# Turning half of the attention probabilities on VectorE and by DMA in the second cross attention of a Perceiver block

## The chip, the cores and the metric

The kernel is one program on one core of a Trainium2 chip. The metric is device time in microseconds (us) of one execution. It is written in float32 and computes six layers one behind another; the change is in the fourth.

## The reference

The input is `x`, 128 batches of 32 tokens with 128 features, and a context of 128 batches of 257 rows. Six layers add to `x`; the one that is changed is the second cross attention. Layer normalisation of `x` gives the queries, keys and values come from the raw context, there are 16 heads of 8 features.

```python
Q = _split_heads(x_q @ W_q.T + b_q)          # x_q = layernorm(x): 128 x 32 x 128
K = _split_heads(x_k @ W_k.T + b_k)          # x_k = x_v = ctx_1024: 128 x 257 x 128
V = _split_heads(x_v @ W_v.T + b_v)
scores = jnp.einsum('bhqd,bhkd->bhqk', Q, K) / jnp.sqrt(jnp.float32(D_K))
scores = jnp.where(mask == 0, jnp.float32(-1000000000.0), scores)
attn = jax.nn.softmax(scores, axis=-1)
out = jnp.einsum('bhqk,bhkd->bhqd', attn, V)
...
return out @ W_o.T + b_o
```

## The kernel before

`xattn1` (from L1424) is the stage. After a short part that makes all queries, a pipeline runs over the 128 batches, one batch to a step. `run_steps` unrolls the first and last steps and loops over the rest, eight steps to a turn of the loop. Each engine has its own `step(g, j)`, with s = 8g + j the step's number; four steps are a tile of 128 tokens and b = j % 4 is the step's place in its tile. The order on an engine is the order in which `step` is written; engines wait for each other by counting semaphores.

One batch has 32 queries and 16 heads, that is 512 rows of scores. They lie as four groups of 128 partitions (4 heads by 32 queries), so the probabilities `prob` of a batch are 128 partitions by 4 groups by 257 keys. To multiply them by the values, the keys have to be on the partitions: the probabilities are turned. The work on batch n is spread over several steps, so in step s:

- TensorE (PE): `turn` (L1732) transposes the probabilities of batch s against the identity into PSUM, four groups for keys 0 to 127 into `turn_ps[0]` and four for keys 128 to 255 into `turn_ps[1]`; then the transposes of `weight` and of the raw context of batch s+4 into `in_ps`; `score` (L1721) for batch s+2; the keys (L1777) of batch s+3 into `turn_ps[0]` and its values (L1782) into `turn_ps[1]`; once a tile the output projection (L1789); last `values` (L1738) for batch s, four matmuls for each half of the keys, accumulated in `out_ps` on top of `last_part`, the share of key 256.
- VectorE (DVE): copies `turn_ps[0]` to `probT[:, 0]` (L1641); the reciprocals `rinv` of batch s+1 (L1646), for which it waits until all four exponentials of batch s+1 are done; if b is 0 the sum over heads `oT_sum` (L1650), if b is 2 the addition to `x` (L1655) and its statistics (L70); then `mask` (L1627) for groups 0 and 1 of batch s+2, which adds the mask to the scores and takes the minimum; `kT` (L1665) of batch s+3; `mask` for groups 2 and 3; and `own` (L1675), which picks each head's part of the output.
- ScalarE (ACT): copies `turn_ps[1]` to `probT[:, 1]` (L1693) and `in_ps` to `turned_in` (L1698); the exponentials of groups 0 and 1 of batch s+2 (L1686); the copy of the values `v` (L1707); the exponentials of groups 2 and 3. An exponential is two instructions, the second reads the row sum.
- GpSimd (POOL): the share of the last key (L1607) and `weight` (L1611) of batch s+1, and once a tile the queries spread over heads (L1594) and the mask as numbers (L1621).
- SyncE (SP): the DMAs. One `b_raw` of 128 KB a step (L1557), `b_kept` (L1561) and `b_v_rows` (L1565) once a tile each.

`turn_ps[1]` is shared: `turn(g, j, 1)` has to wait until ScalarE has copied `v` of the step before out of it (`v_ready`). `turn_ps[0]` is shared in the same way with the keys (`k_ready`).

Of the kernel before, what the change touches and what calls it, by code (L numbers as in the profile page):

```python
# [21 lines left out]
ACT = mybir.ActivationFunctionType  # L22
# [3 lines left out]
P = 128  # L26
# [1397 lines left out]
def xattn1(k, io):  # L1424
# [8 lines left out]
    with ExitStack() as stack:  # L1433
# [87 lines left out]
        rsum, rinv = sb("b_rsum", [P, 4, GROUPS]), sb("b_rinv", [P, 4, GROUPS])  # L1521
        probT = sb("b_probT", [P, 2, CH])
        last_part = sb("b_last_part", [P, 2, D])
# [5 lines left out]

        turn_ps = [psum("b_turn0"), psum("b_turn1")]  # L1530
        out_ps, in_ps = psum("b_out"), psum("b_in")
# [5 lines left out]
        scored, masked, exped, rinv_ready = (sem(f"b_{n}") for n in ("scored", "masked", "exped", "rinv_ready"))  # L1537
        turned, probT_ready = [sem(f"b_turned{n}") for n in range(2)], [sem(f"b_probT_ready{n}") for n in range(2)]
        out_ready, weight_ready, last_ready, own_ready, sum_ready, oT_ready, proj_ready, x_added = (
# [12 lines left out]
        with nc.Block() as block:  # L1552

            @block.sync
            def _(sp):
                def load_raw(g, j):
                    sp.dma_start(raw[:, j % 8], io["ctx_1024"][ds(g * 8 + j, 1), 0:2 * P, :].rearrange(  # L1557
                        "b (t p) d -> p (b t) d", p=P)).then_inc(raw_loaded[j % 8], 16)

                def load_kept(t, u):  # L1560
                    sp.dma_start(kept[:, u], k.keep1[ds(t * BPT, BPT), :].unsqueeze(0).broadcast_to([P, BPT, N_CTX]))\  # L1561
                        .then_inc(kept_loaded[u], 16)

# [62 lines left out]
            def _(dve):  # L1626
                def mask(g, j, grp):  # L1627
                    s, n, par = g * 8 + j, (j + 2) % 8, j % 2
                    if grp == 0:
# [5 lines left out]
                        scalar=3.4e38, op0=ALU.add, op1=ALU.min, accum_out=nmax[:, par, grp:grp + 1]).then_inc(masked, 1)  # L1635

                def step(g, j):
                    s, t, u, b = g * 8 + j, tile_of(g, j), j // 4, j % 4
                    if live(g, j, 0):
                        dve.wait_ge(turned[0], s + 1)  # L1640
                        nc.vector.tensor_copy(probT[:, 0, :], turn_ps[0][:]).then_inc(probT_ready[0], 1)  # L1641
                    if live(g, j, 1):
# [18 lines left out]
                    if live(g, j, 3):  # L1661
                        n = (j + 3) % 4
                        dve.wait_ge(k_done, s + 4)
                        dve.wait_ge(kept_loaded[(j + 3) // 4 % 2], (g + (j + 3) // 8 + 1) * 16)
                        nc.vector.scalar_tensor_tensor(kT[:, n, :], turn_ps[0][:, 0:N_CTX], k.bk1, kept[:, (j + 3) // 4 % 2, n, :],  # L1665
                                                       ALU.add, ALU.mult).then_inc(k_ready, 1)
# [15 lines left out]
            def _(act):  # L1682
# [6 lines left out]
                def step(g, j):  # L1689
                    s, t, u, b = g * 8 + j, tile_of(g, j), j // 4, j % 4  # L1690
                    if live(g, j, 0):
                        act.wait_ge(turned[1], s + 1)
                        nc.scalar.activation(probT[:, 1, :], turn_ps[1][:], ACT.Copy).then_inc(probT_ready[1], 1)  # L1693
                    if live(g, j, 4) or live(g, j, 0):
# [10 lines left out]
                    if live(g, j, 3):  # L1705
                        act.wait_ge(v_done, s + 4)
                        nc.scalar.activation(v[:, (j + 3) % 8], turn_ps[1][:, 0:2 * P].rearrange("p (t d) -> p t d", d=D), ACT.Copy)\  # L1707
                            .then_inc(v_ready, 1)
# [11 lines left out]
            def _(pe):  # L1720
# [10 lines left out]

                def turn(g, j, kt):  # L1732
                    for grp in range(GROUPS):
                        last = nc.tensor.transpose(turn_ps[kt][:, grp * P:(grp + 1) * P],  # L1734
                                                   prob[:, j % 4, grp, kt * P:(kt + 1) * P], k.ident[:])
                    last.then_inc(turned[kt], 1)

                def values(g, j, kt):  # L1738
                    s = g * 8 + j
                    pe.wait_ge(probT_ready[kt], s + 1)  # L1740
                    for grp in range(GROUPS):
                        rows = slice(grp * 32, grp * 32 + 32)
                        last = nc.tensor.matmul(out_ps[rows, 0:P], v[:, j, kt, rows], probT[:, kt, grp * P:(grp + 1) * P],
                                                start=False, stop=(kt == 1), skip_group_check=True)
                    return last

                def step(g, j):
                    s, t, u, b = g * 8 + j, tile_of(g, j), j // 4, j % 4
                    here, ahead = live(g, j, 0), live(g, j, 4)
                    if here:  # L1750
                        pe.wait_ge(exped, s * 4 + 4)
                        pe.wait_ge(k_ready, upto(g, s, 3))
                        turn(g, j, 0)
                        pe.wait_ge(v_ready, upto(g, s, 3))
                        turn(g, j, 1)
                    if here or ahead:
# [12 lines left out]
                    if live(g, j, 3):  # L1769
                        n = (j + 3) % 8  # L1770
                        pe.wait_ge(in_copied, s + 4)
                        if n % 4 == 0:
                            pe.wait_ge(keys_ready, tile_of(g, j, 3) + 1)
                        if here:
                            pe.wait_ge(probT_ready[0], s + 1)
                        wait(pe, k_ready, s + 3)
                        nc.tensor.matmul(turn_ps[0][:, 0:N_CTX], k.wk1[:], turned_in[:, n, C0:C0 + N_CTX], start=True, stop=True).then_inc(k_done, 1)  # L1777
                        if here:
                            pe.wait_ge(probT_ready[1], s + 1)
                        wait(pe, v_ready, s + 3)  # L1780
                        for kt in range(2):
                            last = nc.tensor.matmul(turn_ps[1][:, kt * D:(kt + 1) * D], turned_in[:, n, C0 + kt * P:C0 + (kt + 1) * P], k.wv1[:],  # L1782
                                                    start=True, stop=True)
# [746 lines left out]
```

## Time and profile before

| what | us |
|---|---|
| median of three runs | 2270.99 |
| lowest and highest run | 2270.51, 2272.9 |
| span of the profiled execution | 2270.1 |
| PE, DVE, ACT, POOL busy over the span | 1957.3, 1626.0, 1640.6, 899.0 |
| pipeline of the stage: first to last `b_rinv` | 1336.5 to 1825.5 |

The span is that of one profiled execution; the runs are timed without the profiler. Rows of a timeline have the start, the duration, the engine, the line, the operation, output and inputs, a count, and in brackets the idle time before it and what ended it. Start times of neighbours on one engine tell more than durations, because instructions overlap a little.

### The profile page before, as it was taken

Reading aid. Unit: us, or ns where it says so; the run is one execution under the profiler, and the core shown is the slowest. Engines: PE = TensorE matmul, PEld = TensorE weight load, DVE = VectorE, ACT = ScalarE, POOL = GpSimd, SP = SyncE. Lnnn points to the kernel's source line nnn. Section 1 sums busy time; section 2 is a strip of 40 time slices with the busy share of each in tenths; the row PEclk is TensorE's granted clock in tenths of the full one; section 3 lists DMA queues with packets and bytes.
Section 4 is the critical chain, followed back from the end, with each engine's and each line's share of the span. In section 5 each row is a group of like instructions: output and inputs, shape, how many; then the busy total and the mean of one; then the engine's idle time right before and its main releaser. Section 6 shows DMA issues by size and latency. Waiting matters only on the chain. (4 is left out here: it accounts for less than half of the span.)

```text
span 2270.1 us, 55792 instructions
## 1 busy us (share of the span) xinstructions
PE 1957.3 (86%) x15563; PEld 1549.6 (68%) x15563; DVE 1626.0 (72%) x5153; ACT 1640.6 (72%) x4441; POOL 899.0 (40%) x1338
## 2 busy tenths in 40 slices
PE   3799999999999999995350579999999989858997
PEld 3688888888888888883240257777777756526775
DVE  5677777777777777764778758888888878854564
ACT  3588888888888888876486368888888878735553
POOL 1533443444433333422245123333333357533554
PEclk8699999999999999997585789999999999969999
DMA  4211111111110111100000022222222100013222
GB/s 134 73 34 34 33 33 33 33 33 33 29 28 27 30 33 33 33 4 1 0 0 0 0 73 66 74 65 65 74 65 65 52 2 0 1 28 84 89 83 84
DMA packets 124106, 93.89 MB, mean 41 GB/s; under 512 B 14417, under 2 KB 101937, under 8 KB 123905
## 3 DMA queue, kind: packets, MB, share of 16 engines
q1 hardware_dynamic: 122550, 90.88, 14.6%
q10 hardware_dynamic: 1194, 1.58, 0.2%
q8 instruction: 34, 0.56, 0.1%
q0 software_dynamic: 288, 0.56, 0.1%
q14 instruction: 40, 0.32, 0.0%
HBM read 88.26 MB, written 4.72 MB: 41 GB/s over the span
## 5 line engine op out<-in xcount | busy, mean ns | idle before, releaser
L750 ACT ACTIVATE a_prob<-a_neg,a_nmax 128x289 f32<-128x289 f32 x512 | 270.5, 530 | 79.0 <-DVE a_nmax L679 72.9
L1686 ACT ACTIVATE b_prob<-b_neg,b_nmax 128x257 f32<-128x257 f32 x512 | 255.2, 500 | 71.2 <-DVE b_nmax L1633 71.1
L645 POOL TENSOR_TENSOR a_xn<-a_z,g 128x256 f32<-128x256 f32 x128 | 93.3, 729 | 526.3 <-DVE a_z L705 526.3
L807 PE MATMUL a_score<-a_xnT,a_qT 128*128 128x290 f32 x1536 | 274.8, 315 | 1.1 <-DVE a_qT L726 1.1
L835 PE MATMUL a_out<-a_probT,a_xn 128*128 128x256 f32 x1024 | 263.6, 380 | 0.3 <-DVE a_probT L690 0.3
L679 DVE CUSTOM_DVE_ANT_0 a_neg<-a_score,a_bias 128x289 f32<-128x289 f32 x512 | 222.0, 459 | 46.4 <-PE a_score L807 40.0
L807 PEld LDWEIGHTS a_score<-a_xnT,a_qT 128*128 128x128 f32 x1536 | 216.5, 191 | 43.8 <-issue 43.2
L1633 DVE CUSTOM_DVE_ANT_0 b_neg<-b_score,b_bias 128x257 f32<-128x257 f32 x512 | 195.9, 421 | 50.8 <-PE b_score L1729 48.6
L755 ACT ACTIVATE a_prob<-a_prob,a_rinv 128x256 f32<-128x256 f32 x512 | 230.4, 499 | 1.1 <-DVE a_rinv L717 1.0
L835 PEld LDWEIGHTS a_out<-a_probT,a_xn 128*128 128x128 f32 x1024 | 175.0, 191 | 13.6 <-DVE a_probT L690 0.6
L1607 POOL TENSOR_TENSOR b_last_part<-b_v_rows,b_prob 128x128 f32<-128x128 f32 x128 | 52.0, 406 | 318.2 <-ACT b_prob L1686 318.2
L735 DVE TENSOR_TENSOR a_xnT<-a_ctx,a_xnT 128x256 fp32r<-128x256 f32 x128 | 54.4, 425 | 159.7 <-ACT a_xnT L786 159.7
L2396 POOL TENSOR_TENSOR m_hidden<-m_full,m_hidden 128x512 fp32r<-128x512 f32 (+1 forms) x88 | 114.2, 1298 | 107.2 <-ACT m_hidden L2377 107.2
L1734 PE MATMUL b_turn<-ident,b_prob 128*128 128x128 f32 x1024 | 144.5, 281 | 1.4 <-DVE b_kT L1665 0.7
L854 PE MATMUL a_q<-latT,A 128*128 (+1 forms) x1024 | 139.8, 281 | 6.4 <-DVE a_qT L726 4.1
L854 PEld LDWEIGHTS a_q<-latT,A 128*128 128x128 f32 x1024 | 131.2, 197 | 7.8 <-DVE a_qT L726 5.1
L817 PE MATMUL a_turn<-ident,a_prob 128*128 128x128 f32 x1024 | 132.7, 273 | 0.8 <-ACT a_prob L755 0.7
L1734 PEld LDWEIGHTS b_turn<-ident,b_prob 128*128 128x128 f32 x1024 | 108.9, 141 | 33.5 <-ACT b_prob L1686 14.4
L876 PE MATMUL a_ctx<-U,a_oT 128*128 128x128 f32 x1024 | 119.7, 275 | 0.7 <-ACT a_oT L791 0.7
L817 PEld LDWEIGHTS a_turn<-ident,a_prob 128*128 128x128 f32 x1024 | 118.8, 141 | 1.4 <-ACT a_prob L755 1.4
L2372 ACT ACTIVATE m_silu<-m_g 128x512 f32<-128x512 f32 (+1 forms) x88 | 52.6, 598 | 90.2 <-PE m_g L2026 90.2
L876 PEld LDWEIGHTS a_ctx<-U,a_oT 128*128 128x128 f32 x1024 | 116.9, 192 | 1.1 <-ACT a_oT L791 1.1
(479 smaller groups left out, 5192.2 us busy)
## 6 DMA issues: line engine op xcount, KB each, us to landing
a_raw<-in_ctx SPq DMA_DIRECT2D x128, 128.0 KB, 3.4
b_raw<-in_ctx SPq DMA_DIRECT2D x128, 128.0 KB, 3.3
m_wide<-expert_weights SPq DMA_DIRECT2D x128, 128.0 KB, 2.9
a_kept<-keep SPq DMA_DIRECT2D x32, 257.0 KB, 3.9
b_kept<-keep SPq DMA_DIRECT2D x32, 257.0 KB, 3.5
b_v_rows<-ctx_tail_values SPq DMA_DIRECT2D x32, 256.0 KB, 3.6
a_tail<-latents_normalised SPq DMA_DIRECT2D x64, 64.0 KB
latents_normalised<-lat_affine SPq DMA_DIRECT2D x8, 256.0 KB, 2.3
```

What stands on the lines that cost most here:

```text
L679: nc.vector.tensor_tensor_reduce(out=neg[:, grp, :], in0=score_ps[grp % 2][:, 0:KEYS0], in1=bias[:, n, :], scale=-DH0 ** -0.5, scalar=3.4e ...
L750: nc.scalar.activation(prob[:, par, grp, :], neg[:, grp, :], ACT.Exp, bias=nmax[:, par, grp:grp + 1], scale=-1.0, accum_out=rsum[:, par, g ...
L755: return nc.scalar.activation(part, part, ACT.Copy, scale=rinv[:, (j + 1) % 2, grp:grp + 1])
L807: last = nc.tensor.matmul(score_ps[grp % 2][:, 0:even(KEYS0)], qT[:, a, un, bn, 4 * grp:4 * grp + 4, :], xnT[:, c, n, :], start=(p == 0), ...
L817: last = nc.tensor.transpose(turn_ps[kt][:, grp * P:(grp + 1) * P], prob[:, j % 2, grp, kt * P:(kt + 1) * P], k.ident[:])
L835: nc.tensor.matmul(out_ps[:, half, 0:2 * P], xn[:, j, kt, :], probT[:, kt, half * 2 * P:(half + 1) * 2 * P], start=(kt == 0), stop=False)
L854: last = nc.tensor.matmul(q_ps[:, h * P:(h + 1) * P], k.A[:, 4 * hg + h, :], k.latT[:, ds((t + ahead) * P, P)], start=True, stop=True)
L876: last = nc.tensor.matmul(proj_ps, oT[:, h, :], k.U[:, h, :], start=(h == 0), stop=(h == H - 1))
L1633: nc.vector.tensor_tensor_reduce(out=neg[:, par, grp, :], in0=score_ps[grp][:, 0:N_CTX], in1=bias[:, n, :], scale=-DH1 ** -0.5, scalar=3.4 ...
L1686: nc.scalar.activation(prob[:, n, grp, :], neg[:, par, grp, :], ACT.Exp, bias=nmax[:, par, grp:grp + 1], scale=-1.0, accum_out=rsum[:, n, ...
L1734: last = nc.tensor.transpose(turn_ps[kt][:, grp * P:(grp + 1) * P], prob[:, j % 4, grp, kt * P:(kt + 1) * P], k.ident[:])
L2396: nc.gpsimd.tensor_tensor(h[0:r1, LO, :], full[0:r1, 1 - u, :], h[0:r1, HI, :], ALU.subtract).then_inc(lo_ready, 1)
```

## The change

For keys 0 to 127 the four transposes on TensorE and VectorE's copy of them go. In their place VectorE transposes the 16 blocks of 32 by 32 of the probabilities in SBUF with one instruction (`turn_blocks`), and SyncE issues four DMAs of 64 KB that spread each head's 32 partitions over all 128 (`spread_prob`). The key with the number 4c + r goes through row c of block r, so VectorE reads `prob` with a distance of four elements (16 bytes) between neighbours, and writes runs of 32. This is done for batch s+1 in step s, ahead of the reciprocals. Keys 128 to 255 stay as they were. The keys' projection gets a PSUM bank of its own (`k_ps`), and TensorE's waits for VectorE's copy go.

```diff
-        probT = sb("b_probT", [P, 2, CH])
+        blocks, spreadT = sb("b_blocks", [P, 2, 4, GROUPS, L]), sb("b_spreadT", [P, 2, 4, GROUPS, L])
+        probT = sb("b_probT", [P, CH])
...
+                def spread_prob(g, j):
+                    s, n = g * 8 + j, (j + 1) % 2
+                    sp.wait_ge(blocks_ready, s + 2)
+                    wait(sp, out_ready, s)
+                    for i in range(4):
+                        sp.dma_start(spreadT[:, n, i].rearrange("p g l -> p (g l)"),
+                                     blocks[i * L:(i + 1) * L, n].rearrange("c r g l -> c r (g l)")).then_inc(spreadT_loaded[n], 16)
+
...
+                    if live(g, j, 1):
+                        spread_prob(g, j)
...
+                def turn_blocks(g, j):
...
+                    s, n = g * 8 + j, (j + 1) % 2
+                    dve.wait_ge(exped, s * 4 + 8)
+                    wait(dve, out_ready, s)
+                    nc.vector.transpose(blocks[:, n].rearrange("p r g l -> p g r l"),
+                                        prob[:, (j + 1) % 4, :, 0:P].rearrange("p g (c r) -> p g r c", r=4)).then_inc(blocks_ready, 1)
+
...
-                    if live(g, j, 0):
-                        dve.wait_ge(turned[0], s + 1)
-                        nc.vector.tensor_copy(probT[:, 0, :], turn_ps[0][:]).then_inc(probT_ready[0], 1)
+                    if live(g, j, 1):
+                        turn_blocks(g, j)
...
                 def values(g, j, kt):
-                    s = g * 8 + j
-                    pe.wait_ge(probT_ready[kt], s + 1)
+                    if kt == 0:
+                        pe.wait_ge(spreadT_loaded[j % 2], (g * 4 + (j // 2 + 1)) * 64)
+                    else:
+                        pe.wait_ge(probT_ready, g * 8 + j + 1)
...
                         pe.wait_ge(exped, s * 4 + 4)
-                        pe.wait_ge(k_ready, upto(g, s, 3))
-                        turn(g, j, 0)
                         pe.wait_ge(v_ready, upto(g, s, 3))
-                        turn(g, j, 1)
+                        turn(g, j)
```

VectorE, from the end of a step to the first mask of the next, a step with b = 2. The ISA rows on L1633 (L1645 after) are the mask and the read of its minimum. Before:

```order
L1675 TENSOR_TENSOR b_own<-b_out,b_turned_in 128x128
L1641 COPY b_probT<-b_turn 128x512
L1646 RECIPROCAL b_rinv<-b_rsum 128x4
L1655 TENSOR_TENSOR x<-b_out,x 128x128
L70 BN_STATS stats<-x 128x6
L1633 ISA b_neg,b_nmax<-b_score,b_bias 128x257
```

After:

```order
L1695 TENSOR_TENSOR b_own<-b_out,b_turned_in 128x128
L1655 STREAM_TRANSPOSE b_blocks<-b_prob 128x4x4x32
L1666 RECIPROCAL b_rinv<-b_rsum 128x4
L1675 TENSOR_TENSOR x<-b_out,x 128x128
L70 BN_STATS stats<-x 128x6
L1645 ISA b_neg,b_nmax<-b_score,b_bias 128x257
```

The block transpose stands where the copy stood; it reads `prob` of batch s+1, which ScalarE writes, and no longer a PSUM bank that TensorE writes.

TensorE, one step, before:

```order
L1734 MATMUL b_turn<-ident,b_prob 128x128 x8
L1760 MATMUL b_in<-ident,b_weight 128x128
L1765 MATMUL b_in<-ident,b_raw 128x128 x2
L1729 MATMUL b_score<-b_kT,b_qbd 128x257 x4
L1777 MATMUL b_turn<-b_turned_in,wk1T 128x257
L1782 MATMUL b_turn<-wv1T,b_turned_in 128x128 x2
L1795 MATMUL b_out<-ident,b_last_part 128x128
L1743 MATMUL b_out<-b_probT,b_v 32x128 x8
```

After:

```order
L1754 MATMUL b_turn<-ident,b_prob 128x128 x4
L1780 MATMUL b_in<-ident,b_weight 128x128
L1785 MATMUL b_in<-ident,b_raw 128x128 x2
L1749 MATMUL b_score<-b_kT,b_qbd 128x257 x4
L1795 MATMUL b_k<-b_turned_in,wk1T 128x257
L1800 MATMUL b_turn<-wv1T,b_turned_in 128x128 x2
L1813 MATMUL b_out<-ident,b_last_part 128x128
L1764 MATMUL b_out<-b_spreadT,b_v 32x128 x4
L1764 MATMUL b_out<-b_probT,b_v 32x128 x4
```

Four transposes are gone at the head of the step, and the first four of `values` take `spreadT`.

SyncE, a step with b = 1, before:

```order
L1557 DMA b_raw<-in_ctx 128x2x128
L413 ISA
L1561 ISA
L1561 DMA b_kept<-keep 128x1028
L413 REGISTER_ALU
```

After:

```order
L1559 DMA b_raw<-in_ctx 128x2x128
L1572 REGISTER_ALU
L1575 DMA b_spreadT<-b_blocks 128x1x128 x4
L413 ISA
L1563 ISA
L1563 DMA b_kept<-keep 128x1028
```

The four DMAs stand between a step's `b_raw` and the tile's loads.

## Rows read from the trace of the kernel before

**Rows 1.** Windows: busy us of each engine, granted PE clock, DMA share, GB/s.
```profile
1160.00:1170.00 10.00, 7.15 (x32) 5.60 (x30) 8.63 (x5) 7.14 (x13) 1.29 (x1) 1.00 0.00 0
1500.00:1800.00 300.00, 299.58 (x3310) 224.40 (x3303) 252.80 (x991) 256.96 (x875) 108.83 (x234) 1.00 0.26 67
1970.00:1980.00 10.00, 7.98 (x145) 4.79 (x143) 8.28 (x22) 6.09 (x15) 3.13 (x2) 1.00 0.01 2
1990.00:2000.00 10.00, 8.73 (x32) 5.72 (x32) 7.60 (x28) 4.18 (x8) 0.00 (x0) 0.50 0.00 0
```

**Rows 2.** Waits, 1360 to 1800 us: total us, times, longest.
```profile
ACT b_prob L1686 <- DVE b_nmax L1633: 63.2, 114, 0.8
DVE b_neg L1633 <- PE b_score L1729: 40.8, 58, 0.7
...
PEld b_turn L1734 <- ACT b_v L1707: 2.5, 15, 0.2
```

**Rows 3.** Timeline of ScalarE: the first exponential of five steps in a row.
```profile
1599.56 0.51 ACT L1686 ACTIVATE b_prob<-b_neg,b_nmax 128x257 f32<-128x257 f32 x1 [0.57 <-DVE b_nmax L1633]
...
1603.45 0.51 ACT L1686 ACTIVATE b_prob<-b_neg,b_nmax 128x257 f32<-128x257 f32 x1 [0.69 <-DVE b_nmax L1633]
...
1607.20 0.51 ACT L1686 ACTIVATE b_prob<-b_neg,b_nmax 128x257 f32<-128x257 f32 x1 [0.25 <-DVE b_nmax L1633]
...
1611.16 0.51 ACT L1686 ACTIVATE b_prob<-b_neg,b_nmax 128x257 f32<-128x257 f32 x1 [0.64 <-DVE b_nmax L1633]
...
1614.93 0.51 ACT L1686 ACTIVATE b_prob<-b_neg,b_nmax 128x257 f32<-128x257 f32 x1 [0.57 <-DVE b_nmax L1633]
```

**Rows 4.** Timeline: last row sum of a batch to the next mask, b = 0.
```profile
1601.72 0.19 ACT L1686 ACTIVATION_READ_ACCUMULATOR b_prob<-b_neg,b_nmax 128x1 f32 x1
...
1601.94 0.18 DVE L1646 RECIPROCAL b_rinv<-b_rsum 128x4 f32<-128x4 f32 x1
...
1602.04 1.04 DVE L1650 TENSOR_REDUCE b_oT_sum<-b_own 128x128 f32<-128x512 f32 x1
...
1603.00 0.42 DVE L1633 CUSTOM_DVE_ANT_0 b_neg<-b_score,b_bias 128x257 f32<-128x257 f32 x1
```

**Rows 5.** Timeline of VectorE: reciprocals and first mask, b = 2.
```profile
1609.71 0.17 DVE L1646 RECIPROCAL b_rinv<-b_rsum 128x4 f32<-128x4 f32 x1
...
1610.69 0.43 DVE L1633 CUSTOM_DVE_ANT_0 b_neg<-b_score,b_bias 128x257 f32<-128x257 f32 x1
```

**Rows 6.** Timeline: `v` copy, transposes and VectorE's copy at a step's head.
```profile
1612.16 0.36 ACT L1707 ACTIVATE b_v<-b_turn 128x256 f32<-128x256 f32 x1
1612.16 1.09 PE L1734 MATMUL b_turn<-ident,b_prob 128*128 128x128 f32 x8
...
1612.86 0.69 DVE L1641 COPY b_probT<-b_turn 128x512 f32<-128x512 f32 x1
...
1613.09 0.27 PE L1760 MATMUL b_in<-ident,b_weight 128*128 128x128 f32 x1
...
1613.54 0.18 DVE L1646 RECIPROCAL b_rinv<-b_rsum 128x4 f32<-128x4 f32 x1
```

**Rows 7.** Groups of VectorE over 512 elements: busy us, mean ns, idle.
```profile
L1650 DVE TENSOR_REDUCE b_oT_sum<-b_own 128x128 f32<-128x512 f32 x32 | 33.4, 1045 | 0.0
...
L1908 DVE TENSOR_REDUCE s_rsum<-s_expd 128x16 f32<-128x512 f32 x32 | 21.5, 671 | 0.2
```

**Rows 8.** The DMAs of L1557 and the one of 64 KB: duration, landing.
```profile
L1557 SPq DMA_DIRECT2D b_raw<-in_ctx x128: 372/373/470, 1324.1 to 1790.9; - x128
...
DMA to landing us min/median/max: 2.6/3.3/5.2
...
ctx_tail_values<-b_v_tail SPq DMA_DIRECT2D x1, 64.0 KB, 1.6
```

**Rows 9.** The last reciprocals and the last `values` of the pipeline.
```profile
1825.49 0.18 DVE L1646 RECIPROCAL b_rinv<-b_rsum 128x4 f32<-128x4 f32 x1 [0.39 <-ACT b_prob L1686]
...
1828.21 0.77 PE L1743 MATMUL b_out<-b_probT,b_v 128*32 128x128 f32 x16
```

More of the change, by code:

```diff
@@ L1528, in xattn1 @@
         score_ps = [psum(f"b_score{g}") for g in range(GROUPS)]
-        turn_ps = [psum("b_turn0"), psum("b_turn1")]
+        k_ps, turn_ps = psum("b_k"), psum("b_turn")
         out_ps, in_ps = psum("b_out"), psum("b_in")
@@ L1537, in xattn1 @@
         scored, masked, exped, rinv_ready = (sem(f"b_{n}") for n in ("scored", "masked", "exped", "rinv_ready"))
-        turned, probT_ready = [sem(f"b_turned{n}") for n in range(2)], [sem(f"b_probT_ready{n}") for n in range(2)]
+        turned, probT_ready = sem("b_turned"), sem("b_probT_ready")
+        blocks_ready, spreadT_loaded = sem("b_blocks_ready"), [sem(f"b_spreadT_loaded{u}") for u in range(2)]
         out_ready, weight_ready, last_ready, own_ready, sum_ready, oT_ready, proj_ready, x_added = (
@@ L1664, in step @@
                         dve.wait_ge(kept_loaded[(j + 3) // 4 % 2], (g + (j + 3) // 8 + 1) * 16)
-                        nc.vector.scalar_tensor_tensor(kT[:, n, :], turn_ps[0][:, 0:N_CTX], k.bk1, kept[:, (j + 3) // 4 % 2, n, :],
+                        nc.vector.scalar_tensor_tensor(kT[:, n, :], k_ps[:, 0:N_CTX], k.bk1, kept[:, (j + 3) // 4 % 2, n, :],
                                                        ALU.add, ALU.mult).then_inc(k_ready, 1)
@@ L1691, in step @@
                     if live(g, j, 0):
-                        act.wait_ge(turned[1], s + 1)
-                        nc.scalar.activation(probT[:, 1, :], turn_ps[1][:], ACT.Copy).then_inc(probT_ready[1], 1)
+                        act.wait_ge(turned, s + 1)
+                        nc.scalar.activation(probT[:], turn_ps[:], ACT.Copy).then_inc(probT_ready, 1)
                     if live(g, j, 4) or live(g, j, 0):
@@ L1706, in step @@
                         act.wait_ge(v_done, s + 4)
-                        nc.scalar.activation(v[:, (j + 3) % 8], turn_ps[1][:, 0:2 * P].rearrange("p (t d) -> p t d", d=D), ACT.Copy)\
+                        nc.scalar.activation(v[:, (j + 3) % 8], turn_ps[:, 0:2 * P].rearrange("p (t d) -> p t d", d=D), ACT.Copy)\
                             .then_inc(v_ready, 1)
@@ L1730, in score, with turn @@
                     last.then_inc(scored, 1)
-                def turn(g, j, kt):
+                def turn(g, j):
                     for grp in range(GROUPS):
-                        last = nc.tensor.transpose(turn_ps[kt][:, grp * P:(grp + 1) * P],
-                                                   prob[:, j % 4, grp, kt * P:(kt + 1) * P], k.ident[:])
-                    last.then_inc(turned[kt], 1)
+                        last = nc.tensor.transpose(turn_ps[:, grp * P:(grp + 1) * P], prob[:, j % 4, grp, P:2 * P], k.ident[:])
+                    last.then_inc(turned, 1)
                 def values(g, j, kt):
-                    s = g * 8 + j
-                    pe.wait_ge(probT_ready[kt], s + 1)
+                    if kt == 0:
+                        pe.wait_ge(spreadT_loaded[j % 2], (g * 4 + (j // 2 + 1)) * 64)
+                    else:
+                        pe.wait_ge(probT_ready, g * 8 + j + 1)
                     for grp in range(GROUPS):
                         rows = slice(grp * 32, grp * 32 + 32)
-                        last = nc.tensor.matmul(out_ps[rows, 0:P], v[:, j, kt, rows], probT[:, kt, grp * P:(grp + 1) * P],
+                        last = nc.tensor.matmul(out_ps[rows, 0:P], v[:, j, kt, rows],
+                                                spreadT[:, j % 2, :, grp, :] if kt == 0 else probT[:, grp * P:(grp + 1) * P],
                                                 start=False, stop=(kt == 1), skip_group_check=True)
@@ L1773, in step @@
                             pe.wait_ge(keys_ready, tile_of(g, j, 3) + 1)
+                        wait(pe, k_ready, s + 3)
+                        nc.tensor.matmul(k_ps[:, 0:N_CTX], k.wk1[:], turned_in[:, n, C0:C0 + N_CTX], start=True, stop=True).then_inc(k_done, 1)
                         if here:
[L1775 to L1779, printed above, removed]
+                            pe.wait_ge(probT_ready, s + 1)
                         wait(pe, v_ready, s + 3)
                         for kt in range(2):
-                            last = nc.tensor.matmul(turn_ps[1][:, kt * D:(kt + 1) * D], turned_in[:, n, C0 + kt * P:C0 + (kt + 1) * P], k.wv1[:],
+                            last = nc.tensor.matmul(turn_ps[:, kt * D:(kt + 1) * D], turned_in[:, n, C0 + kt * P:C0 + (kt + 1) * P], k.wv1[:],
                                                     start=True, stop=True)
```

## The prediction

> **What bounds the kernel now.** I read the windows first. In the pipeline of the stage TensorE looks full: 299.58 of 300 us busy at a granted clock of 1.00 [rows 1]. That alone would say that four transposes fewer a batch are pure gain. So I read the waits next [rows 2]: ScalarE waits in each step for VectorE's minimum (63.2 us in 114 steps), VectorE in half of the steps for TensorE's scores (40.8 us in 58), and TensorE at times for ScalarE's copy of `v` (2.5 us in 15). Each of the three waits for another, so the thing to look for is closed loops that pass through several engines. I measure a step from one first exponential to the next [rows 3]: 3.89 us into b = 0, 3.75 into b = 1, 3.96 into b = 2, 3.77 into b = 3; together 15.37, 3.84 a batch. Two loops matter.
>
> *Loop 1, ScalarE and VectorE.* From the first exponential (1599.56 [rows 3]) to the end of the last row sum of the batch is 2.35 us (1601.72 + 0.19 [rows 4]). 0.03 later come the reciprocals, 0.10 after their start the sum over heads, 0.96 after that the first mask (1603.00), and 0.45 later the first exponential of the next step. That is 3.89, exactly the step into b = 0: there VectorE is never idle, and this loop is the bound. Without the sum over heads the same loop is 2.35 + 0.03 + 0.10 + 0.47 = 2.95. With b = 2 the addition to `x` and its statistics stand between reciprocals and mask, 0.98 instead of 0.10 [rows 5], so it is 3.83.
>
> *Loop 2, through all three.* The `v` copy starts 1.00 us after the first exponential and ends at 1612.52; TensorE's eight transposes start at 1612.16 and the next transpose follows at 1613.09, that is 0.117 each [rows 6]. The fifth, the first that needs `v` to be out of its bank, is due at 1612.63, only 0.11 after the copy ends. TensorE's queue and this loop are thus almost equally long; the queue decides the steps into b = 1, 2 and 3 (3.96 is the one with the projection in it).
>
> **What the change takes away.** Four transposes are 4 x 0.117 = 0.47 us of TensorE's queue. But in loop 2 little of it comes back: the four that stay may start when the copy ends, 1612.52 + 0.03, they need 0.47, and the next transpose stands at 1613.02 instead of 1613.09. The loop is 3.77 - 0.07 = 3.70. So the gain is at most 0.07 in an ordinary step, and in the step into b = 2, where the projection no longer shows, 3.96 - 3.70 = 0.26. VectorE's copy goes too; it took 0.68 from start to start [rows 6], but it ran while VectorE was waiting for the last exponential anyhow (1612.86 to 1613.54, with the row sum done only shortly before).
>
> **What it adds on VectorE.** The block transpose of batch s+1 needs all four exponentials of that batch, as the reciprocals do, and stands ahead of them. It can't start before the last row sum, and behind it in VectorE's queue stand the reciprocals, the extra work and the first mask, for which ScalarE waits. So its whole time T goes into loop 1, in every step. This is the new wait: an operation that waited for a bank that was ready early is replaced by one that waits for the latest event of the step. The loops become 2.95 + T (b = 1 and 3), 3.89 + T (b = 0) and 3.83 + T (b = 2).
>
> How long is T? No block transpose is in the trace. The low bound is the copy of the same 512 elements, 0.68. The nearest row that reads SBUF at a distance is the sum over heads, also 512 elements, neighbours 32 elements apart: it takes 1045 ns against 671 for a sum over as many contiguous elements [rows 7], and 0.96 from start to start [rows 4]. The transpose reads four elements apart. I take 0.96, since that row shares the unusual thing, the distance, and keep 0.68 for the low end. The high end is half the copy's rate, 2 x 0.68 = 1.36, my estimate.
>
> The pages disagree here. The Trainium skill (SBUF — State Buffer, the note on cachelines) says that SBUF is read in lines of 16 bytes and that each access that goes on to a new line pays; reads 16 bytes apart do so each time, which would give the slow value and 2339 us; it also names four fp32 as how far one may stride for free, which is just this distance, so it can be read either way. The Trainium skill (Vector Engine (DVE) Microarchitecture Reference, on `transpose_mode`) says that the 32x32 transpose sustains one element per cycle per lane, which would give the fast value and 2308 us. Rows 7 fit the first for a sum and show nothing of a transpose.
>
> **What it adds as DMA.** Four issues a batch on SyncE; an issue takes 0.37 and, with what lies between, about 0.42 [rows 8], so the last starts 1.3 us after the blocks are ready. One of 64 KB landed in 1.6, those of 128 KB in 3.3 as a median [rows 8]. The last lands 2.9 to 4.6 after the blocks. They are used by the last matmuls of the next step; counted only to the next first mask that is one loop and what stands between transpose and mask, at least 3.91 + 0.98 or 4.79 + 0.10, 4.89 us. So they are hidden. Behind the four in SyncE's queue stand loads needed steps later. At the end there is no cover: the last batch's blocks are ready at 1825.49 + 0.96, its `values` start at 1828.21 [rows 9] and would start at 1829.3 to 1831.1. I count 2 us.
>
> **The sum.** 2 x 3.91 + 4.85 + 4.79 = 17.46 a tile, 4.365 a batch, against 3.84: +0.52. Over 127 steps 66 us, and the end 2: +68. The profiled execution's span is 2270.1 and the median 2271.0, so 0.9 lies around it and stays: 2271 + 68 = **2339 us**. Each 0.1 of T is worth 12.7 us.
>
> **The rivals.**
> *The transpose costs as the copy does, T = 0.68.* Then b = 1 and 3 are bound by loop 2: 2 x 3.70 + 4.57 + 4.51 = 16.48, 4.12 a batch, +0.28 x 127 + 2 = 37, 2308 us. For it: the engine may not care about distance; the slow row is also a sum of only four terms.
> *It is slower than any row, T up to 1.36.* +0.40 x 127 = 51 more, 2390 us.
> *The DMAs are late, or TensorE's clock falls.* If the longest landing, 5.2 [rows 8], were the rule, the blocks would come after 6.5 instead of 4.9 us; 1.6 x 127 is 200 more, above 2500. If TensorE, now idle about a fifth of each step, were granted 0.50 (1.2 of 2.4 GHz), the part of loop 2 between `v` being out (1612.55, 1.39 after the first exponential) and the first mask (0.47 before the next) would double: 3.70 - 1.39 - 0.47 = 1.84 more, 5.5 a step, near 2490. Against it: windows with 72 and 80% busy kept 1.00, and only after long gaps did one stand at 0.50 [rows 1].
> *Not slower: the transposes were the bound after all.* TensorE's queue is 0.47 shorter, at most 60 us, 2211. For this loop 1 must stay below 3.84 on average. Its mean is (2 x 2.95 + 3.89 + 3.83) / 4 + T = 3.41 + T, so T must be under 0.43, two elements a cycle, and loop 2 must be looser than I read it, under some 3.4. With T = 0.34 and loop 2 out of the way a step is 3.75, 12 us less, with the end 2261. If only T is so short and loop 2 stays at 3.70, it is (2 x 3.70 + 4.23 + 4.17) / 4 = 3.95, 2287, still slower.
>
> **How the numbers follow.** T near 0.96: 50%, 2325 to 2355. T near the copy's: 24%, down to 2300. T from 1.06 to 1.36: 16%, up to 2390. Late DMAs or a lower clock: 5%, above. Not slower: 5%. The range 2300 to 2390 holds the first three. A measurement of this kernel can tell about 0.2%, 4.5 us, from no change: faster by more than that 3%, within it 2%, slower 95%.
>
> **What would show it.** The step, from first exponential to first exponential, should be near 3.9, 4.8, 3.9 and 4.85. VectorE should wait for ScalarE ahead of the block transpose in every step, and hardly any more for the scores; ScalarE's wait for the minimum should grow from 0.55 to about 1.1 a step; TensorE should wait at its four transposes for `v` and show gaps, at a clock of 1.00. `values` should wait for no DMA until the last batch. I am wrong if the transpose starts without an idle time before it, if it takes under 0.45, or if TensorE still shows no gap.

## The result, and the profile after

| | before | after |
|---|---|---|
| median of the timed runs, us | 2271.55 | 2340.99 |
| lowest and highest run | 2270.51, 2272.9 | 2340.25, 2342.31 |
| ratio, 95% interval | | 1.0303 [1.0289, 1.0318] |
| span of the profiled execution | 2270.1 | 2339.5 |
| first to last `b_rinv` of the pipeline | 489.0 | 553.8 |
| mean step | 3.85 | 4.36 |

The medians are of four runs each; those of the kernel before hold one run more than the table ahead of the prediction. The mean step is the distance from first to last `b_rinv`, divided by the 127 steps. The change costs 69 us, and the loop bound that the prediction worked out is what sets the step. The first view to compare is the timeline of ScalarE over one tile; these rows answer to [rows 3].

```profile
1600.14 0.51 ACT L1706 ACTIVATE b_prob<-b_neg,b_nmax 128x257 f32<-128x257 f32 x1 [0.71 <-DVE b_nmax L1645]
...
1605.03 0.51 ACT L1706 ACTIVATE b_prob<-b_neg,b_nmax 128x257 f32<-128x257 f32 x1 [1.69 <-DVE b_nmax L1645]
...
1608.96 0.51 ACT L1706 ACTIVATE b_prob<-b_neg,b_nmax 128x257 f32<-128x257 f32 x1 [0.44 <-DVE b_nmax L1645]
```

The distances, with those of the next two steps (first exponentials at 1613.70 and 1617.62), and the mean of the kernel before over 1400 to 1780 us:

| step into | before | predicted | after |
|---|---|---|---|
| b = 0 | 3.96 | 4.85 | 4.89 |
| b = 1 | 3.75 | 3.91 | 3.93 |
| b = 2 | 3.96 | 4.79 | 4.74 |
| b = 3 | 3.77 | 3.91 | 3.92 |

The mean before for b = 0 hides two values. The step is 3.89 in one tile and 4.02 in the next, in turn; the five rows of [rows 3] hold the short one. The long one, from 1614.93 to 1618.95, is the first step of a turn of the loop over eight steps. In the kernel after, both kinds of tile have 4.9. The four steps before thus sum to 15.44 and not 15.37, 3.86 a batch.

Now the inside of the step into b = 0, from the last row sum of the batch to the next first exponential; it answers to [rows 4].

```profile
1602.30 0.19 ACT L1706 ACTIVATION_READ_ACCUMULATOR b_prob<-b_neg,b_nmax 128x1 f32 x1
...
1602.52 1.13 DVE L1655 STREAM_TRANSPOSE b_blocks<-b_prob 128x512 f32<-128x512 f32 x1 [0.78 <-ACT b_prob L1706]
1603.55 0.16 DVE L1666 RECIPROCAL b_rinv<-b_rsum 128x4 f32<-128x4 f32 x1
1603.60 1.05 DVE L1670 TENSOR_REDUCE b_oT_sum<-b_own 128x128 f32<-128x512 f32 x1
1604.53 0.46 DVE L1645 CUSTOM_DVE_ANT_0 b_neg<-b_score,b_bias 128x257 f32<-128x257 f32 x1
```

The transpose starts 0.03 us after the row sum's end (1602.49). Ahead of it VectorE stood idle for 0.78 us, and from its start to the mask VectorE never stops. The four parts are 1.03, 0.05, 0.93 and, to the exponential at 1605.03, 0.50. With the 2.38 from the first exponential to the transpose they are 4.89: the loop closes, with nothing of TensorE in it.

The groups of the page tell the same of the whole run.

```profile
L1706 ACT ACTIVATE b_prob<-b_neg,b_nmax 128x257 f32<-128x257 f32 x512 | 255.1, 500 | 137.6 <-DVE b_nmax L1645 137.5
...
L1655 DVE STREAM_TRANSPOSE b_blocks<-b_prob 128x512 f32<-128x512 f32 x128 | 143.4, 1120 | 98.8 <-ACT b_prob L1706 98.8
L1645 DVE CUSTOM_DVE_ANT_0 b_neg<-b_score,b_bias 128x257 f32<-128x257 f32 x512 | 195.4, 423 | 2.5 <-PE b_score L1749 2.5
...
L1754 PE MATMUL b_turn<-ident,b_prob 128*128 128x128 f32 x512 | 81.4, 282 | 117.3 <-ACT b_v L1727 117.3
```

ScalarE now waits 137.5 us for the minimum, 1.07 a batch. VectorE waits 98.8 us for the last exponential, always at the transpose, and hardly any more for scores: 2.5 us, where [rows 2] had 40.8 in the stretch up to 1800 us. TensorE waits 117.3 us for the `v` copy. The window of the middle of the pipeline (columns as in [rows 1]) shows how much room that leaves:

```profile
1400.00:1800.00 400.00, 313.97 (x3526) 225.24 (x3525) 322.10 (x1167) 299.77 (x1032) 132.57 (x274) 1.00 0.49 120
```

TensorE is busy for 314 of 400 us at a granted clock of 1.00 to two digits. In that window there is one exception: from 1626 to 1629 us the granted clock was 0.50 (1.2 GHz, the lower of its two levels), and the step that starts at 1626.41 took 5.39 instead of 4.75, 0.64 us more; the keys' two matmuls took 1.03 us at 1625.53 and 0.70 at 1630.62. The engine that looked full in [rows 1] now has 86 us of gaps, and the kernel is slower.

The DMAs: ahead the issues on SyncE's queue, with the use of what they bring; behind them the page's row with the median landing; last the waits of TensorE from 1360 to 1860 us that name them.

```profile
1603.68 2.49 SPq L1575 DMA_DIRECT2D b_spreadT<-b_blocks  x4
...
1609.47 0.43 PE L1764 MATMUL b_out<-b_spreadT,b_v 128*32 128x128 f32 x8
```

```profile
b_spreadT<-b_blocks SPq DMA_DIRECT2D x512, 64.0 KB, 2.2
```

```profile
PEld b_out L1764 <- DMA b_spreadT<-b_blocks: 0.8, 3, 0.3
```

The four issues take 2.49 us, some 0.62 each. The fourth starts about 1.87 after the first, 1605.55, and lands with the median 2.2 at 1607.75. The blocks were ready at about 1603.6, so the chain is 4.1 to 4.2 us long. The matmul that reads the blocks starts at 1609.47, 1.7 us later. TensorE waited for these DMAs 3 times in 114 steps, for 0.8 us together.

### The profile page after: what moved, and what is told of

It reads as the page before. It is cut to its first block and busy times, and to the rows that moved or that the text cites. A ratio compares the mean times of both kernels' runs of the same rounds, so it can differ in the third digit from the quotient of the medians.

```text
span 2339.5 us, 55599 instructions
## 1 busy us (share of the span) xinstructions
PE 1906.0 (81%) x15051; PEld 1497.3 (64%) x15051; DVE 1659.9 (71%) x5153; ACT 1637.8 (70%) x4441; POOL 904.8 (39%) x1338
## 5 line engine op out<-in xcount | busy, mean ns | idle before, releaser
L1706 ACT ACTIVATE b_prob<-b_neg,b_nmax 128x257 f32<-128x257 f32 x512 | 255.1, 500 | 137.6 <-DVE b_nmax L1645 137.5
L1655 DVE STREAM_TRANSPOSE b_blocks<-b_prob 128x512 f32<-128x512 f32 x128 | 143.4, 1120 | 98.8 <-ACT b_prob L1706 98.8
L1645 DVE CUSTOM_DVE_ANT_0 b_neg<-b_score,b_bias 128x257 f32<-128x257 f32 x512 | 195.4, 423 | 2.5 <-PE b_score L1749 2.5
L1754 PE MATMUL b_turn<-ident,b_prob 128*128 128x128 f32 x512 | 81.4, 282 | 117.3 <-ACT b_v L1727 117.3
L1754 PEld LDWEIGHTS b_turn<-ident,b_prob 128*128 128x128 f32 x512 | 54.1, 142 | 148.4 <-ACT b_prob L1706 137.2
L854 PEld LDWEIGHTS a_q<-latT,A 128*128 128x128 f32 x1024 | 130.9, 196 | 8.2 <-DVE a_qT L726 5.5
```

What stands on the lines that cost most here:

```text
L854: last = nc.tensor.matmul(q_ps[:, h * P:(h + 1) * P], k.A[:, 4 * hg + h, :], k.latT[:, ds((t + ahead) * P, P)], start=True, stop=True)
L1645: nc.vector.tensor_tensor_reduce(out=neg[:, par, grp, :], in0=score_ps[grp][:, 0:N_CTX], in1=bias[:, n, :], scale=-DH1 ** -0.5, scalar=3.4 ...
L1655: nc.vector.transpose(blocks[:, n].rearrange("p r g l -> p g r l"), prob[:, (j + 1) % 4, :, 0:P].rearrange("p g (c r) -> p g r c", r=4)).t ...
L1706: nc.scalar.activation(prob[:, n, grp, :], neg[:, par, grp, :], ACT.Exp, bias=nmax[:, par, grp:grp + 1], scale=-1.0, accum_out=rsum[:, n, ...
```

## The experiments

Each kernel was timed beside the kernel before (2271.5, 2271.9 and 2272.0 us in three groups). The mean step is again the distance from first to last `b_rinv` over 127; single steps in the text are repeated values from the middle of the pipeline.

| kernel | us | ratio, 95% interval | mean step |
|---|---|---|---|
| no DMAs | 2339.29 | 1.0304 [1.0287, 1.0321] | 4.36 |
| neither transposes nor DMAs | 2272.56 | 1.0005 [0.9995, 1.0015] | 3.86 |
| contiguous reads | 2306.76 | 1.0157 [1.014, 1.0174] | 4.10 |
| block transpose twice | 2473.32 (one run) | | 5.39 |
| tile work ahead | 2295.11 | 1.0102 [1.0086, 1.0117] | 4.00 |
| contiguous, tile work ahead | 2276.76 | 1.0019 [1.0009, 1.0028] | 3.85 |
| the same, inputs first on TensorE | 2260.69 | 0.9944 [0.9931, 0.9958] | 3.74 |
| kernel before in these orders | 2280.06 | 1.0031 [1.0021, 1.0041] | 3.91 |
| the one before last, sum late | 2256.10 | 0.9933 [0.9919, 0.9946] | 3.70 |
| the same without DMAs | 2243.17 | 0.9875 [0.986, 0.9891] | 3.61 |

### Are the DMAs part of it?

```diff
-                    if live(g, j, 1):
-                        spread_prob(g, j)
...
-                        pe.wait_ge(spreadT_loaded[j % 2], (g * 4 + (j // 2 + 1)) * 64)
+                        pe.wait_ge(spreadT_loaded[0], 1)
...
+                nc.vector.memset(spreadT[:], 0.0).then_inc(spreadT_loaded[0], 1)
```

> The changed kernel without the four DMAs of each batch: VectorE still turns the blocks, but spreadT is zeroed once and TensorE multiplies zeros for keys 0 to 127 (that part of the attention is left out). Loop theory (the time is the block transpose, 1.04 us from start to start, in the loop of ScalarE and VectorE): the step stays as it is, only the uncovered end of the pipeline goes, 2337 to 2341 us. Rival, late or disturbing DMAs (their issues take 2.5 us of each step on SyncE and the DMA share is 0.49): it falls clearly, towards 2310 us or below.

2339.29 us, 1.7 below the changed kernel. Its steps are 4.87, 3.91, 4.75 and 3.91, those of the changed kernel within 0.02, and from first to last `b_rinv` it takes 553.6 us, the changed kernel 553.8. The 512 DMAs cost nothing in the steps. What is left fits the 2 us counted for the end of the pipeline: behind the last `b_rinv` come 444.2 us here and 447.1 in the changed kernel.

### Is it the block transpose, and what were four transposes fewer worth?

The edit before, and VectorE's transpose goes as well.

```diff
-                    if live(g, j, 1):
-                        turn_blocks(g, j)
```

> Neither the block transpose nor the DMAs; spreadT is zeroed once, so keys 0 to 127 are left out of the attention; TensorE's four transposes and VectorE's copy stay removed. Loop theory: only what loops 1 and 2 of the prediction give back, (2 x 3.70 + 3.89 + 3.83) / 4 = 3.78 us a batch against 3.84, 8 us less than before: 2263 us. Rival, TensorE's queue was the bound: 0.47 us a batch less, 2211 us.

2272.56 us, no different from the kernel before. So the block transpose alone makes the 67 us between this kernel and the one without DMAs. But the 2263 that my theory expected didn't come either: TensorE does 0.47 us less a batch, VectorE has lost its copy, and nothing is won. The rival, by which TensorE's queue alone was the bound (2211), falls with it. The steps are 3.96 into b = 0 (3.9 and 4.03 in turn), 3.81, 3.88 and 3.81. The timeline of a step into b = 1, from its `v` copy on, tells why.

```profile
1605.61 0.36 ACT L1724 ACTIVATE b_v<-b_turn 128x256 f32<-128x256 f32 x1
...
1606.12 0.63 PE L1751 MATMUL b_turn<-ident,b_prob 128*128 128x128 f32 x4 [0.54 <-ACT b_v L1724]
...
1606.58 0.27 PE L1777 MATMUL b_in<-ident,b_weight 128*128 128x128 f32 x1
...
1607.00 0.72 PE L1746 MATMUL b_score<-b_kT,b_qbd 32*128 32x257 f32 x8
...
1607.95 0.43 DVE L1643 CUSTOM_DVE_ANT_0 b_neg<-b_score,b_bias 128x257 f32<-128x257 f32 x1 [0.78 <-PE b_score L1746]
```

The step begins with the exponential at 1604.61, 1.00 ahead of the copy, and ends with the next at 1608.41, 0.46 behind the mask. The `v` copy ends at 1605.97 and the transposes start 0.15 later, not 0.03, after TensorE has stood idle for 0.54. The next transpose comes 0.61 after the copy's end; in the kernel before it came 0.57 after it [rows 6]. The four transposes that are gone were done while `v` was not out yet; without them TensorE stands idle for that time, and what follows comes no earlier. Loop 2, added up from these rows, is 1.00 + 0.36 + 0.15 + 0.46 + 0.42 + 0.95 + 0.46 = 3.80 us, where I had 3.70 and the kernel before 3.75 [rows 3].

### Is it the distance of the reads?

VectorE reads each block as 32 neighbours. The keys then come in another order, which the projection of the keys and the mask are given too.

```diff
-                                        prob[:, (j + 1) % 4, :, 0:P].rearrange("p g (c r) -> p g r c", r=4)).then_inc(blocks_ready, 1)
+                                        prob[:, (j + 1) % 4, :, 0:P].rearrange("p g (r c) -> p g r c", r=4)).then_inc(blocks_ready, 1)
...
-                        nc.tensor.matmul(k_ps[:, 0:N_CTX], k.wk1[:], turned_in[:, n, C0:C0 + N_CTX], start=True, stop=True).then_inc(k_done, 1)
+                        nc.tensor.matmul(k_ps[:, 0:P], k.wk1[:], turned_in[:, n, C0:C0 + P].rearrange("p (c r) -> p r c", r=4),
+                                         start=True, stop=True)
+                        nc.tensor.matmul(k_ps[:, P:N_CTX], k.wk1[:], turned_in[:, n, C0 + P:C0 + N_CTX], start=True, stop=True).then_inc(k_done, 1)
```

> The changed kernel with the keys in an order in which VectorE reads each block of 32 as contiguous elements: TensorE makes the keys' columns in that order (one matmul more a batch) and the mask is stored in it. If the 16 bytes between the elements cost the time, the transpose takes about 0.68 us from start to start like a copy, b = 1 and 3 are bound by loop 2, and the whole is near 2308 us. Rival, the time lies in the transpose itself: it stays at 1.04 us and the whole at 2341 us.

The page's group of the transpose:

```profile
L1657 DVE STREAM_TRANSPOSE b_blocks<-b_prob 128x512 f32<-128x512 f32 x128 | 91.0, 711 | 86.2 <-ACT b_prob L1708 86.2
```

```profile
1602.52 0.71 DVE L1657 STREAM_TRANSPOSE b_blocks<-b_prob 128x512 f32<-128x512 f32 x1 [0.65 <-ACT b_prob L1708]
1603.16 0.14 DVE L1668 RECIPROCAL b_rinv<-b_rsum 128x4 f32<-128x4 f32 x1
```

711 ns instead of 1120, and 0.64 instead of 1.03 from start to start. The steps into b = 0 and b = 2 fall by 0.42 and 0.40, to 4.47 and 4.34; those into b = 1 and 3 only to 3.81, which is loop 2. That makes 2306.76 us, half of the loss. The rival "as the copy does", 2308, was thus right for another kernel: 512 elements do take 0.64, if they lie side by side. That the time agrees to 1 us is in part luck: the steps into b = 1 and 3 are 0.11 longer than that rival had them, the other two 0.10 and 0.17 shorter. The Trainium skill (SBUF — State Buffer, the note on cachelines) lets each access that goes on to a new 16-byte line pay. These two kernels agree: at a distance of exactly 16 bytes the price is 0.4 us for 512 elements. The prediction's other reading of that note, by which four fp32 are free, does not hold here.

### Does its whole time go into the step?

```diff
+                    nc.vector.transpose(again[:, n].rearrange("p r g l -> p g r l"),
+                                        prob[:, (j + 1) % 4, :, 0:P].rearrange("p g (c r) -> p g r c", r=4))
```

> The changed kernel with the block transpose done twice in a row, the first into a buffer that nobody reads. Loop theory: each step grows by the whole 1.04 us, 127 x 1.04 = 132 us, 2473 us. Rival, part of the transpose lies beside other waits: clearly less than 132 us more.

```profile
L1656 DVE STREAM_TRANSPOSE b_again<-b_prob 128x512 f32<-128x512 f32 x128 | 142.5, 1114 | 80.2 <-ACT b_prob L1709 77.6
...
L1658 DVE STREAM_TRANSPOSE b_blocks<-b_prob 128x512 f32<-128x512 f32 x128 | 136.2, 1064 | 0.0
```

2473.32 us, and the median steps are 5.84, 4.89, 5.74 and 4.90, each 0.96 to 0.99 longer than in the changed kernel (4.88, 3.91, 4.75, 3.91). The second transpose takes 0.98 from start to start (1502.91 to 1503.89 in one step), so nothing of it is hidden, in any place of the tile. That the whole comes out at the expected 132 us more is in part luck. Between first and last `b_rinv` the granted clock was 0.88 on average, against 1.00 in the changed kernel. Steps of 6.4 to 6.8 us stand where it was lowest (0.66 to 0.74 over 10 us), and the pipeline grew by 130.9 us, where 127 times 0.98 is 124.

### Can the idle time ahead of the transpose be used?

VectorE has 0.78 us of idle time there, while the sum over heads (b = 0) and the addition to `x` with its statistics (b = 2) stand behind it. Both are moved ahead of it.

```diff
-                    if live(g, j, 1):
-                        turn_blocks(g, j)
                     if b == 0 and live(g, j, -1):
...
                     if b == 2 and live(g, j, -4):
...
+                    if live(g, j, 1):
+                        turn_blocks(g, j)
```

> The changed kernel with VectorE's work of once a tile (the sum over heads, the addition to x and its statistics) moved from behind the reciprocals to ahead of the block transpose, where VectorE waits 0.78 us a step for the last exponential. Loop theory: loop 1 then holds only the transpose, 2.35 + 0.03 + 1.04 + 0.05 + 0.46 = 3.93 us in every step, with about 0.1 more at b = 0; 3.96 a batch against 3.85 before, 127 x 0.11 + 2 = 16 us more than before, 2287 us. Rival, VectorE's total work is what counts and its place does not: 2341 us.

2295.11 us: 46 of the 69 come back, 8 us short of the expected 2287. Three of four steps are 3.91 to 3.92, loop 1 with nothing but the transpose in it. The one with b = 0 is 4.14 and 4.22 in turn, because the sum is 1.0 us long, starts after `own`, and ends after the last exponential.

The same with contiguous reads:

> The move of the tile's work and the contiguous key order together. Loop 1 is 3.53 us (3.65 at b = 0), so all steps are bound by loop 2 through the copy of v, measured at 3.81 us in the kernels without its cover: 127 x (3.81 - 3.85) + 2, 2268 us, level with before. Rival, that something else holds the 3.81 us steps (then it may come out either way, above 2275 or below 2260 us).

2276.76 us, 9 above what was expected. Three steps are 3.79 to 3.81, loop 2 at the size that the runs before had shown. The one with b = 0 was expected at 3.81 too; it is 3.87 and 4.14 in turn, 4.00 on average, which makes 6 of the 9 us. The rest lies ahead of the pipeline, whose first `b_rinv` comes at 1339.8 instead of 1336.5.

### Can loop 2 be shortened?

TensorE waits for `v` at the head of its step. The transposes of the inputs, which don't need it, are put ahead of `turn`, on top of the last edit.

```diff
-                    if here:
-                        pe.wait_ge(exped, s * 4 + 4)
-                        pe.wait_ge(v_ready, upto(g, s, 3))
-                        turn(g, j)
...
                         last.then_inc(in_turned, 1)
+                    if here:
+                        pe.wait_ge(exped, s * 4 + 4)
+                        pe.wait_ge(v_ready, upto(g, s, 3))
+                        turn(g, j)
                     if live(g, j, 2):
```

> As the one before, and on TensorE the transposes of weight and of the raw context moved ahead of the four transposes of the probabilities, so that 0.43 us of its work no longer waits for the copy of v. Loop 2 falls to 3.38 us, then loop 1 (3.53, 3.65 at b = 0) and TensorE's own queue (about 3.5, 3.73 with the projection) bound the steps: near 3.61 a batch, 30 us less than before and 2 for the end, 2243 us. Rival, loop 2 is not what holds the steps at 3.81: no gain over the one before, 2268 us.

2260.69 us, 11 under the kernel before, but 18 above the expected 2243. The steps other than b = 0 are 3.51, 3.73 and 3.56, as expected; b = 0 stays at 3.86 and 4.14, where 3.65 was expected. VectorE's timeline in one of 4.14:

```profile
1610.93 0.29 DVE L1697 TENSOR_TENSOR b_own<-b_out,b_turned_in 128x128 f32<-128x128 f32 x1
1611.53 1.05 DVE L1665 TENSOR_REDUCE b_oT_sum<-b_own 128x128 f32<-128x512 f32 x1 [0.30 <-DVE b_own L1697]
1612.49 0.70 DVE L1657 STREAM_TRANSPOSE b_blocks<-b_prob 128x512 f32<-128x512 f32 x1
1613.12 0.14 DVE L1679 RECIPROCAL b_rinv<-b_rsum 128x4 f32<-128x4 f32 x1
```

The sum waits for `own`, which its own engine writes, and starts 0.60 after it. The transpose has no idle time ahead of it any more: here VectorE is the bound from `own` on. The wait is not always that long. In the next tile `own` starts at 1625.86 and the sum at 1626.18, 0.32 later and with no idle time, and that step takes 3.86. The two alternate all along, with 0.60 in the first step of a turn of the loop over eight steps. So the 0.28 between them go with the turn of the loop and not with the wait for `own` as such; what in the turn costs them was not tested. Six steps that start before 1402 us are longer than their like, 4.1 to 5.2 us, and up to 1403 us TensorE's weight loads waited ten times for the DMAs, 7.3 us in all.

Is that the orders' doing alone? The kernel before, with the same two moves (its copy in the place of the transpose):

> The kernel before, with only the two changes of order (VectorE's work of once a tile first, TensorE's input transposes first), as a control. With all eight transposes and the copy in place TensorE's queue needs about 3.75 us a step (3.97 with the projection) whatever its order: between 2265 and 2272 us. Rival, the order alone brings the gain: near 2243 us.

2280.06 us, 8 slower than before and above both expectations. The steps are 3.76 and 3.91 in turn into b = 0, then 4.15, 3.96 and 3.77, so the loss is in the step into b = 1.

```profile
1605.36 1.06 DVE L1642 TENSOR_REDUCE b_oT_sum<-b_own 128x128 f32<-128x512 f32 x1
1606.33 0.68 DVE L1652 COPY b_probT<-b_turn 128x512 f32<-128x512 f32 x1
...
1607.11 0.67 PE L1777 MATMUL b_turn<-b_turned_in,wk1T 128*128 128x257 f32 x2 [0.34 <-issue]
```

In its timeline the eight transposes end later, VectorE's copy starts behind the sum over heads, and the keys' matmul starts only when that copy is done, since the two share `turn_ps[0]`: TensorE stands idle for 0.34 us ahead of it. The orders alone do not pay. How the 0.40 us of that step come about I read off one place and did not test.

Last, the sum over heads goes between the fourth mask and `own`, where `own` of the step before is long written.

```diff
                     if b == 0 and live(g, j, -1):
...
-                        nc.vector.tensor_reduce(oT_sum[:], own[:].rearrange("p b h l -> p b l h"), AX.X, ALU.add).then_inc(sum_ready, 1)
...
+                        nc.vector.tensor_reduce(oT_sum[:], own[:].rearrange("p b h l -> p b l h"), AX.X, ALU.add).then_inc(sum_ready, 1)
                     if live(g, j, 0):
                         dve.wait_ge(out_ready, s + 1)
                         dve.wait_ge(in_copied, s + 5)
```

> As e7_contig_first_in, with the sum over heads moved once more: from ahead of the block transpose, where it had to wait for own of the same engine and pushed the transpose past the last exponential (steps into b = 0 of 3.86 and 4.14 us), to between the fourth mask and own. There its 0.96 us end 0.1 before the last exponential does. Theory: the steps into b = 0 and b = 1 together fall from 7.5 to about 7.2 us, 32 x 0.35 = 11 us less, 2250 us. Rival, VectorE's queue is simply full in these steps and the order cannot help: 2260 us.

2256.10 us, 16 under the kernel before, and the fastest here of those that leave nothing out. Against the kernel without this move that is some 5 us less, where the theory had 11 and the rival none; neither fits. Waits from 1400 to 1780 us show a name that was all but absent in this stretch:

```profile
PEld b_out L1766 <- DMA b_spreadT<-b_blocks: 14.8, 47, 1.4
...
PE b_out L1766 <- DMA b_spreadT<-b_blocks: 3.4, 13, 1.2
```

So this kernel was run without the DMAs, by the edit of the first experiment:

> The same without the four DMAs a batch, spreadT zeroed once (keys 0 to 127 are left out of the attention). The steps are now 3.5 to 3.7 us and the DMAs need about 1.9 us of issues and 2.2 to land, so the cover is thinner than in the changed kernel. Theory: still covered, 2 us less for the end of the pipeline. Rival, the DMAs have become part of the bound: over 5 us less.

2243.17 us, 13 less; the rival expectation (more than 5 less) holds. Without the DMAs TensorE is busy for all 380 us of that window at a clock of 1.00, with them for 375.9. In the changed kernel the same DMAs were worth 1.7. In the profiled executions the two kernels differ by 13.1 us: 10.7 between first and last `b_rinv` (469.3 and 458.6), 2.0 behind it and 0.4 ahead. Of the 10.7 a good part falls early: up to 1403 us TensorE's weight loads waited eleven times for the DMAs, 6.5 us in all, and four steps are 4.2 to 4.9 us long, where the kernel without DMAs has none of that kind. Whether it is the queue of SyncE (about 2.5 of 3.7 us are spread issues) or the landings that are late was not told apart.

## Why the prediction was right, point by point

**What bounds the kernel.** Right in what it forecast: TensorE was 99.9% busy in [rows 1], and removing four transposes with all that came with them leaves the time where it was. That shows that work taken out of its queue buys nothing, because loop 2 is as long. It does not show which of the two set the steps into b = 1, 2 and 3 before; the prediction's word for the queue there was not tested by itself. The base was read from one tile, the one with the short step into b = 0: 3.84 a batch, where the mean is 3.86.

**The block transpose, T.** Predicted 0.96 from the sum over heads [rows 4, 7]; measured 1.03 to 1.05. The gap from the reciprocals to the next operation was taken as 0.10 and is 0.05. Together they are 1.08 instead of 1.06 a step, so two small errors cancel. The reason for choosing that row, the distance, is borne out: contiguous reads give 0.64. That the sizes are so near is in part luck, since the sum reads 32 elements apart and the transpose four.

**Where it goes.** Wholly into loop 1, in all four steps, as the median steps of the kernel with two transposes show. The four predicted steps sum to 17.46, the measured ones to 17.48.

**The sum.** From first to last `b_rinv` the pipeline grew by 64.8 us, where 66 were predicted; what lies before it grew by 2.1 and what lies behind it by 2.5, together the 69.4 of the spans. The 2 at the end were right in size; the kernels without the DMAs have 444.2 to 444.6 us behind the last `b_rinv`, as the kernel before has (444.6), and those with them 445.3 to 448.0. The last `values` wait 1.04 us for the DMAs:

```profile
1896.55 0.20 PEld L1764 LDWEIGHTS b_out<-b_spreadT,b_v 128*32 128x32 f32 x8 [1.04 <-DMA b_spreadT<-b_blocks]
```

The 2.1 ahead of the pipeline were not in the sum. About half of them is a term that it left out: the first block transpose, 1.03 us, stands ahead of the first `b_rinv`, so T comes 128 times and not 127. The rest is an earlier part of the stage: the first mask starts at 1334.63 instead of 1333.65. That start varies in kernels that hardly differ up to there (1334.20 with neither part, 1336.15 for the contiguous one with the tile work ahead), so it is not shown to come from the change. Of the terms that the prediction did add up, 66 and 2, the runs show 64.8 and 2.5.

**The mis-sized term: loop 2.** 3.70 predicted, 3.80 to 3.81 measured. The reading that failed is "the four that stay may start when the copy ends, 1612.52 + 0.03". I had taken the 0.03 from ScalarE's hand-over to VectorE; from ScalarE to TensorE it is 0.15. With it goes the assumption that the four transposes gone would give back 0.07: the next transpose comes 0.61 after the copy's end instead of 0.57, so loop 2 grew. It did no harm to the forecast, since loop 1 is the longer in all four steps. For the kernel with neither part it is the larger part of the 9.6 us by which the expectation was too low: 0.11 in two of four steps is 7 us. The rest is in the steps into b = 0 and 2, 3.96 and 3.88 where 3.89 and 3.83 were taken.

**The DMAs.** Issue 0.62 instead of 0.42; landing 2.0 to 4.0, with a median of 2.2 that lies between the 1.6 and 3.3 taken. The chain of 4.1 to 4.2 us lies inside the 2.9 to 4.6 of the prediction, under a cover of 4.89, and is hidden, as the kernel without DMAs shows.

**The rivals.** The fast transpose, 2308, was refuted by the 1120 ns, and its mechanism confirmed by the contiguous kernel at 2307. "Late DMAs" was refuted at this step length. The lower clock is there, but only in passing: 0.50 from 1626 to 1629 us cost 0.64 us, and from 1892 on, at the pipeline's end, it was 0.50 again; from 1340 to 1892 us it was 1.00 otherwise. "The transposes were the bound after all" was refuted by the kernel with neither: loop 2, which had to be under 3.4, is 3.80.

## What to carry to other kernels

Taking work out of an engine that is 99.9% busy need not help when three engines wait for each other: follow the chain from one start of an operation to the next start of the same operation, add up each such loop, and ask which loop the edit shortens and which it lengthens. An operation that waits for the latest event of the step and stands ahead of what the next step waits for costs its whole length; move work that is ready early ahead of it, and see that it does not itself wait. What is hidden is hidden at one step length only: the DMAs that cost 1.7 us in all at 4.36 us a step cost 13 at 3.70. And read more than one tile before taking a mean: here every second tile differs.

## What the runs showed of the hardware that was not expected

- Each DMA from SBUF to SBUF of 64 KB took 0.60 to 0.62 us of SyncE's queue; one of 128 KB from HBM took 0.37 [rows 8]. Size alone is not what sets it; the cause was not tested.
- The first matmul of TensorE after a wait for ScalarE starts 0.15 us after ScalarE's end (1606.12 after 1605.97 with neither part; the weight load of it starts at 1606.09), VectorE's transpose 0.03 (1602.52 after 1602.49 in the changed kernel).
- A step in which the loop turns can be longer than its like elsewhere: into b = 0 it is 4.02 against 3.89 us in the kernel before, and 4.14 against 3.86 with the contiguous reads, the tile work ahead and the inputs first. In the changed kernel, where loop 1 is 4.9, the difference is not there.
- The granted clock of TensorE was 1.00 in the pipeline of the changed kernel but for some 3 us, and 0.88 on average in that of the kernel with two block transposes (one execution).
